# The causal mask enters the score banks by copies on ScalarE and VectorE instead of by a product on TensorE

## The chip, the cores and the metric

The kernel runs on one core of a Trainium2 chip. The metric is the device time of one execution in microseconds (us). Before the change the median of three runs is 2950.63 us (2949.73 to 2951.7).

## The reference, cut to what matters

An audio tower: 64 rows of 2048 samples are cut into 128 tokens of 16 samples, embedded into 256 features, passed through an attention that is near the identity, normalised, and then sent through two transformer layers. Each layer has an attention and a feed-forward part. What the change touches is the attention of the two layers, computed per row of 128 tokens with 8 heads of 64:

```python
q, k = rotary_xpos(l2norm(q) * qs, l2norm(k) * ksc)
sim  = einsum('bhwid,bhwjd->bhwij', q * 8, k)       # scores, 128 x 128 per head
sim  = where(i < j, -max, sim)                      # causal mask
attn = softmax(sim);  out = attn @ v;  x = x + out @ wo
```

The 64 rows are independent windows for this kernel: one row is one window of 128 tokens.

## The kernel before, in words

`front` does the tokenizer and the first attention, `layers` the two transformer layers. In `layers` each engine runs a written-out order of work. `attention_tensor`, `attention_scalar`, `attention_vector`, `attention_pool` and `attention_sync` each have a `body(t, i, u, on)`, which is step t. `on(lag)` says that in step t the engine does its part for row b = t - lag. So one step holds parts of six different rows, in a software pipeline: 64 rows and 5 more steps to drain, first peeled steps, then a loop over four steps at a time, then peeled steps again. Engines meet only through counting semaphores; `need(engine, sem, n)` is a wait for a count. Within an engine all is in order.

PSUM has 8 banks. In the layers' attention, banks 0 and 1 take the projection to q and k, bank 2 the projection to v and later the product of weights and values, banks 3 and 4 the transposes (of q and k, later of the softmax weights), banks 5 and 6 are the score banks `ps_s` (four heads of 128 columns in each, index r), bank 7 takes the transposed input and the output projection.

One step, in each engine's own order:

- TensorE: transpose x of row t (L1215); projection to q and k, then v, for row t-1 (L1202 to L1204, 18 products of 512 columns); output projection of row t-5 (L1244 to L1246); transposes of q and k of row t-2 (L1257); weights times values of row t-4 (L1269); the mask product into both score banks (L1279) and the 16 score products (L1284) of row t-2; transposes of the softmax weights of row t-3 (L1294). L1279 multiplies a 128x128 bf16 identity by the bf16 mask `causal` (four copies of a 128x128 pattern with -1e30 above the diagonal) with `start=True`, and the score products add to it with `start=False`.
- ScalarE: copy of transposed x (L948, L949); four exponentials of row t-3, r = 0 (L937, each with a read of its accumulator); squares of q and k of row t-1 (L957); four exponentials, r = 1; copies v (L965), qT (L970), kT (L972), oT_hi (L977), two ET (L983).
- VectorE: low parts of x (L1068, L1070); reciprocal and scaling of the weights r = 0 (L1059, L1061); the rotary products rot_a (L1079) and rot_b (L1082, two); reciprocal and scaling r = 1; x_new (L1095); sum of squares (L1099) and its clamp ssm (L1101); the row maximum of the scores (L1106) and nbias (L1111); oT_lo (L1118).
- GpSimd: adds rot_a and rot_b (L873), the power -1/2 of ssm (L879), scales k (L883).

The score products wait for qT, kT, and for `exp_done`, that is, for the exponentials of the row before, which read the same banks.

Of the kernel before, what the change touches and what calls it, by code (L numbers as in the profile page):

```python
# [11 lines left out]
ACT = mybir.ActivationFunctionType  # L12
# [28 lines left out]
def need(eng, sem, n):  # L41

    if not isinstance(n, int) or n > 0:
        eng.wait_ge(sem, n)
# [548 lines left out]
def run_from(eng, base, count, depth, body):  # L593

    head = -(-(depth + 2) // 4) * 4  # L600

    def peeled(t):
        body(base + t, (base + t) // 4, t % 4, lambda lag: 0 <= t - lag < count)

    for t in range(head):
        peeled(t)
    with eng.Fori(head // 4, count // 4) as i:
        for u in range(4):
            body(4 * i + (base + u), i + base // 4, u, lambda lag: True)
    for t in range(count, count + depth):  # L610
        peeled(t)
# [95 lines left out]
def layers(nc, c, w, q_scale, k_scale, cos, sin, ln_g, ln_b, b1, xa, xb, out, extra):  # L707
# [4 lines left out]
    with ExitStack() as ctx:  # L712
# [14 lines left out]
        oT_hi = m.sb("oT_hi", [P, KI, P], F32R)  # L727
        oT_lo = m.sb("oT_lo", [P, KI, P], F32R)
# [6 lines left out]
        ps_s = banks[:, 5:7]  # L735
# [5 lines left out]
        s = {n: m.sem(n) for n in (  # L741
            "xT_ps", "xT_hi", "xT_lo", "qk_ps", "v_ps", "squared", "normed", "rn_done", "rot_a", "rot_b", "roped",
            "qk_done", "v_done", "q_ps", "k_ps", "qT_done", "kT_done", "s_ps", "top_done", "nbias_done", "exp_done",
            "rsum_done", "en_done", "e_ps", "et_done", "o_ps", "oT_hi", "oT_lo", "out_ps", "x_done")}

        n = Memory(nc, ctx, "ffn")
        w.forward_home(n)
# [168 lines left out]
        def group_high(act, layer, t, u):  # L916
            for kk in range(KD):
                need(act, f["xT_ps"], KD * t + kk + 1)
                need(act, f["xT_lo"], KD * (t - 1) + kk + 1)
                act.activation(yg[:, kk], ps_T[:, kk], ACT.Identity, bias=b_col[:, layer, kk:kk + 1],  # L920
                               scale=g_col[:, layer, kk:kk + 1]).then_inc(f["xg"], 1)
            for kk in range(KD):
                need(act, f["xg"], KD * t + kk + 1)
                need(act, f["h_ps"], KH * (t - 1))
                act.activation(yT_hi[:, u % 2, kk], yg[:, kk], ACT.Copy).then_inc(f["xT_hi"], 1)

        def attention_scalar(act, layer):
            L = layer * ROWS

            def exps(t, u, r):  # L930
                b, slot = t - 3, (u - 3) % 2
                if r == 0:
                    need(act, s["nbias_done"], b + 1)
                    need(act, s["e_ps"], 2 * b)
                for i in range(HEADS // 2):
                    h = 2 * i + r
                    last = act.activation(E[:, r, i], ps_s[:, r, i * P:(i + 1) * P], ACT.Exp,  # L937
                                          bias=nbias[:, r, i:i + 1], scale=rn[:, slot, h:h + 1],
                                          accum_out=sums[:, r, i:i + 1])
                last.then_inc(s["exp_done"], 1)  # L940

            def body(t, i, u, on):
                step = t - L if isinstance(t, int) else None
                if on(0):

                    need(act, s["xT_ps"], t + 1)
                    need(act, s["v_ps"], t - 1)
                    act.activation(xT_hi[:, u % 2, 0], ps_x[:, 0:P], ACT.Copy).then_inc(s["xT_hi"], 1)  # L948
                    act.activation(xT_hi[:, u % 2, 1, 1:P], ps_x[:, P:2 * P - 1], ACT.Copy).then_inc(s["xT_hi"], 1)  # L949
                if on(3):  # L950
                    exps(t, u, 0)
                if on(1):
                    b = t - 1

                    need(act, s["qk_ps"], b + 1)
                    need(act, s["normed"], 2 * b - 1)
                    act.activation(sq[:].rearrange("p h d -> p (h d)"), ps_qk[:].rearrange("p a n -> p (a n)"),  # L957
                                   ACT.Square).then_inc(s["squared"], 1)
                if on(3):
                    exps(t, u, 1)  # L960
                if on(1):
                    b = t - 1
                    need(act, s["v_ps"], b + 1)
                    need(act, s["o_ps"], b - 3)
                    act.activation(v[:, (u - 1) % 4], ps_v[:], ACT.Copy).then_inc(s["v_done"], 1)  # L965
                if on(2):
                    b = t - 2
                    need(act, s["q_ps"], b + 1)
                    need(act, s["s_ps"], b)
                    act.activation(qT[:].rearrange("p k n -> p (k n)"), ps_q[:], ACT.Copy).then_inc(s["qT_done"], 1)  # L970
                    need(act, s["k_ps"], b + 1)
                    act.activation(kT[:].rearrange("p k n -> p (k n)"), ps_k[:], ACT.Copy).then_inc(s["kT_done"], 1)  # L972
                if on(4):
                    b = t - 4
                    need(act, s["o_ps"], b + 1)
                    need(act, s["out_ps"], b)
                    act.activation(oT_hi[:].rearrange("p k n -> p (k n)"), ps_v[:], ACT.Copy).then_inc(s["oT_hi"], 1)  # L977
                if on(3):
                    b = t - 3
                    need(act, s["o_ps"], b)  # L980
                    for r, src in ((0, ps_q), (1, ps_k)):
                        need(act, s["e_ps"], 2 * b + r + 1)
                        act.activation(ET[:, r].rearrange("p i n -> p (i n)"), src[:], ACT.Copy  # L983
                                       ).then_inc(s["et_done"], 1)
                if step == ROWS + 4:
                    group_high(act, layer, layer * GROUPS, 0)

            run_from(act, L, ROWS, 5, body)

        def forward_scalar(act, layer):  # L990
# [60 lines left out]
        def attention_vector(dve, layer):  # L1051
# [3 lines left out]
            def normalise(t, r):  # L1055
                b = t - 3
                need(dve, s["exp_done"], 2 * b + r + 1)
                need(dve, s["en_done"], 2 * b + r - 1)
                dve.reciprocal(rsum[:, r], sums[:, r]).then_inc(s["rsum_done"], 1)  # L1059
                need(dve, s["rsum_done"], 2 * b + r + 1)  # L1060
                dve.tensor_tensor(E[:, r], E[:, r], rsum[:, r].unsqueeze(2).to_broadcast([P, HEADS // 2, P]),  # L1061
                                  ALU.mult).then_inc(s["en_done"], 1)

            def body(t, i, u, on):
                step = t - L if isinstance(t, int) else None
# [8 lines left out]
                if on(1):  # L1074
                    b = t - 1
# [9 lines left out]
                    last.then_inc(s["rot_b"], 1)  # L1085
                if on(3):
                    normalise(t, 1)
                if step == ROWS + 3:
                    group_statistics(dve, layer * GROUPS, layer * GROUPS // 4, 0)
                if on(5):  # L1090
                    b, hf, slot = t - 5, 2 * i + (u - 5) // 2, (u - 5) % 2
# [4 lines left out]
                if on(1):  # L1096
                    b = t - 1
# [4 lines left out]
                if on(2):  # L1102
                    b, slot = t - 2, u % 2
# [11 lines left out]
                if on(4):  # L1115
                    b = t - 4
# [4 lines left out]
                if step == ROWS + 4:  # L1121
                    group_low(dve, layer * GROUPS, 0)

            run_from(dve, L, ROWS, 5, body)

        def forward_vector(dve, layer):
# [70 lines left out]
        def attention_tensor(pe, layer):  # L1197
# [9 lines left out]
            def body(t, i, u, on):  # L1207
                step = t - L if isinstance(t, int) else None
# [8 lines left out]
                if on(1):  # L1217

                    b, slot = t - 1, (u - 1) % 2
# [15 lines left out]
                if on(5):  # L1235

                    b = t - 5
# [10 lines left out]
                if on(2):  # L1248

                    b, slot = t - 2, u % 2  # L1250
# [9 lines left out]
                if on(4):  # L1260

                    b = t - 4
# [9 lines left out]
                if on(2):  # L1272

                    b = t - 2
                    need(pe, s["qT_done"], b + 1)
                    need(pe, s["kT_done"], b + 1)
                    need(pe, s["exp_done"], 2 * b)
                    for r in range(2):
                        pe.matmul(ps_s[:, r], c["ident_b"][:], c["causal"][:].rearrange("p i n -> p (i n)"),  # L1279
                                  start=True, stop=False, skip_group_check=True)  # L1280
                    for j in range(HEADS // 2):
                        for r in range(2):
                            part = slice(r * HD, (r + 1) * HD)
                            last = pe.matmul(ps_s[:, r, j * P:(j + 1) * P], qT[part, j], kT[part, j], start=False,  # L1284
                                             stop=True, skip_group_check=True)
                    last.then_inc(s["s_ps"], 1)
                if on(3):

                    b = t - 3
# [215 lines left out]
```

## Time and profile before

| | |
|---|---|
| median of 3 runs | 2950.63 us |
| the profiled execution's own time | 2949.1 us |
| its span, first to last instruction | 2947.3 us |
| mean granted TensorE clock | 0.974 of full speed |
| TensorE busy | 2735.2 us (93%) |
| VectorE busy | 2028.5 us (69%) |
| ScalarE busy | 1711.5 us (58%) |
| GpSimd busy | 1416.4 us (48%) |

Matrix products are pipelined, so that their durations overlap; what one costs is read from the distance between starts. The two layers' attentions run from about 724 to 1394 us and from about 1837 to 2515 us of the span. A stretch in which an engine has no idle time is one that this engine paces; whether another engine is close behind is read from that engine's idle time and what ended it.

### The profile page before, as it was taken

The page shows a single profiled execution, that of the slowest core. Times are in us where ns is not written, and L with a number is a line of the kernel's source. Part 1 is how long each engine was busy: PE and PEld are TensorE (multiplying, and loading weights), DVE is VectorE, ACT ScalarE, POOL GpSimd, SP SyncE. Part 2 cuts the span into 40 slices and gives each one's busy share as a digit, 9 for nine tenths or more (in the row PEclk, how much of TensorE's full clock was granted, in tenths as well). Part 3 has the DMA queues.
Part 4 walks back from the last instruction along what each step waited for, and adds up shares of the span by engine and source line. Part 5 has one row for each costly group of instructions (what it writes and reads, how often), then busy time and mean ns, then how long its engine had stood idle before and what let it go on. Part 6 is the DMA issues. An engine that isn't in the chain of part 4 may idle for free.

```text
span 2947.3 us, 68736 instructions
## 1 busy us (share of the span) xinstructions
PE 2735.2 (93%) x23808; PEld 2327.5 (79%) x23808; DVE 2028.5 (69%) x3898; ACT 1711.5 (58%) x4309; POOL 1416.4 (48%) x1338
## 2 busy tenths in 40 slices
PE   6998888994999999998799998899999999699998
PEld 5887777883788888887588887688888888588887
DVE  4665555654888888886565554788888888466664
ACT  3555445552777777776344442677777777344443
POOL 7666666665866666664200001866666666000000
PEclk9999999997999999999899999999999999799999
DMA  1000000012111111111211111111111111122221
GB/s 25 30 29 28 28 28 28 31 50 65 42 38 37 37 37 39 40 39 40 73 55 54 53 52 40 44 38 39 40 38 37 37 37 32 54 82 80 76 76 44
DMA packets 149258, 130.57 MB, mean 44 GB/s; under 512 B 23133, under 2 KB 147327, under 8 KB 149100
## 3 DMA queue, kind: packets, MB, share of 16 engines
q1 hardware_dynamic: 146796, 119.87, 13.5%
q0 software_dynamic: 2304, 8.47, 1.0%
q8 instruction: 114, 1.87, 0.3%
q14 instruction: 44, 0.36, 0.0%
HBM read 77.54 MB, written 50.33 MB: 43 GB/s over the span
## 4 chain that ended last, share of the span: by engine, by line
PE 67%; issue 4%; DMA 2%; POOL 1%; DVE 1%; ACT 1%; SPq 0%; DVEq 0%; POOLq 0%; ACTq 0%
PE const_banks L1202 6%; PE const_banks L1204 6%; PE const_banks L1203 6%; PE const_banks L1315 5%; PE const_banks L1317 5%; PE const_banks L1316 5%; PE const_banks L1284 5%; PE const_banks L1294 4%; PE const_banks L1269 4%; PE const_banks L1257 4%; PE const_banks L1329 2%; PE const_banks L1331 2%; PE const_banks L1330 2%; PE const_banks L1279 2%; PE const_banks L1246 2%
## 5 line engine op out<-in xcount | busy, mean ns | idle before, releaser
L873 POOL TENSOR_TENSOR attn_qk<-attn_rot_a,attn_rot_b 128x1024 f32<-128x1024 f32 x128 | 365.0, 2851 | 470.4 <-PE const_banks L1257 364.5
L937 ACT ACTIVATE attn_E<-const_banks,attn_nbias,attn_rn 128x128 f32<-128x128 f32 x1024 | 456.3, 471 | 3.9 <-DVE attn_nbias L1111 3.7
L879 POOL TENSOR_TENSOR attn_rn<-attn_ssm,const_neg_half 128x16 f32<-128x16 f32 x128 | 373.6, 2919 | 16.5 <-DVE attn_ssm L1101 5.5
L860 POOL TENSOR_TENSOR ffn_rstd<-ffn_var,const_neg_half 128x4 f32<-128x4 f32 x32 | 32.3, 1010 | 725.8 <-DVE ffn_var L1036 725.8
L1202 PE MATMUL const_banks<-weights_w_hi,attn_xT_hi 128*128 128x512 f32 x768 | 314.9, 410 | 4.7 <-DVE attn_rot_b L1082 4.1
L1315 PE MATMUL const_banks<-ffn_xT_hi,ffn_w_hi 128*128 128x512 f32 x704 | 283.6, 403 | 25.2 <-DVE ffn_gated L1135 21.6
L1204 PE MATMUL const_banks<-weights_w_hi,attn_xT_lo 128*128 128x512 f32 x768 | 303.1, 395 | 0.0
L1203 PE MATMUL const_banks<-weights_w_lo,attn_xT_hi 128*128 128x512 f32 x768 | 301.0, 392 | 0.0
L1135 DVE SCALAR_TENSOR_TENSOR ffn_gated<-const_banks,ffn_b_col,ffn_gate 128x512 f32<-128x512 f32 (+1 forms) x192 | 143.7, 748 | 225.1 <-ACT ffn_gate L1004 217.7
L1317 PE MATMUL const_banks<-ffn_xT_hi,ffn_w_lo 128*128 128x512 f32 x704 | 279.9, 398 | 0.0
L1316 PE MATMUL const_banks<-ffn_xT_lo,ffn_w_hi 128*128 128x512 f32 x704 | 279.8, 397 | 0.0
L983 ACT ACTIVATE attn_ET<-const_banks 128x512 f32<-128x512 f32 x256 | 139.5, 595 | 210.7 <-PE const_banks L1294 210.7
L1004 ACT ACTIVATE ffn_gate<-const_banks,ffn_b_col 128x512 f32<-128x512 f32 x160 | 110.0, 688 | 228.9 <-PE const_banks L1317 228.8
L937 ACT ACTIVATION_READ_ACCUMULATOR attn_E<-const_banks,attn_nbias,attn_rn 128x1 f32 x1024 | 224.5, 219 | 0.0
L1061 DVE TENSOR_TENSOR attn_E<-attn_E,attn_rsum 128x512 f32<-128x512 f32 x256 | 209.9, 820 | 8.8
L1014 ACT ACTIVATE ffn_h_hi<-ffn_gated 128x512 fp32r<-128x512 f32 x160 | 101.2, 632 | 158.8 <-DVE ffn_gated L1135 158.8
L1329 PE MATMUL const_banks<-ffn_w_hi,ffn_h_hi 128*128 128x256 f32 x640 | 182.0, 284 | 6.1 <-DVE ffn_h_lo L1143 6.1
L1331 PE MATMUL const_banks<-ffn_w_hi,ffn_h_lo 128*128 128x256 f32 x640 | 181.5, 284 | 0.0
L1330 PE MATMUL const_banks<-ffn_w_lo,ffn_h_hi 128*128 128x256 f32 x640 | 181.5, 284 | 0.0
L1079 DVE TENSOR_TENSOR attn_rot_a<-const_banks,attn_cos_s 128x1024 f32<-128x1024 f32 x128 | 156.6, 1224 | 34.7 <-ACT attn_sq L957 33.6
L1315 PEld LDWEIGHTS const_banks<-ffn_xT_hi,ffn_w_hi 128*128 128x128 f32 x704 | 134.2, 191 | 52.5 <-DVE ffn_gated L1135 22.5
L368 ACT ACTIVATE ident_E<-const_banks 128x1024 f32<-128x1024 f32 x128 | 124.1, 1022 | 83.4 <-PE const_banks L551 83.4
(171 smaller groups left out, 7945.9 us busy)
## 6 DMA issues: line engine op xcount, KB each, us to landing
attn_x_<-xa SPq DMA_DIRECT2D x128, 128.0 KB, 2.1
attn_x_res<-xa SPq DMA_DIRECT2D x128, 128.0 KB, 2.1
xb<-attn_x_new SPq DMA_DIRECT2D x128, 128.0 KB, 1.7
ffn_x_<-xb SPq DMA_DIRECT2D x32, 512.0 KB
h<-ident_h SPq DMA_DIRECT2D x64, 128.0 KB, 1.7
xa<-ident_n SPq DMA_DIRECT2D x64, 128.0 KB, 1.7
xa<-ffn_x_new SPq DMA_DIRECT2D x16, 512.0 KB, 3.6
ffn_add<-h SPq DMA_DIRECT2D x16, 512.0 KB, 7.0
```

Of the source, the lines that this page charges most:

```text
L873: pool.tensor_tensor(qk[:, slot].rearrange("p a n -> p (a n)"), rot_a[:].rearrange("p a h d -> p (a h d)"), rot_b[:].rearrange("p a h d -> ...
L879: pool.tensor_tensor(rn[:, slot], ssm[:], c["neg_half"][:], ALU.pow).then_inc(s["rn_done"], 1)
L937: last = act.activation(E[:, r, i], ps_s[:, r, i * P:(i + 1) * P], ACT.Exp, bias=nbias[:, r, i:i + 1], scale=rn[:, slot, h:h + 1], accum_o ...
L1202: pe.matmul(out_, xT_hi[:, slot, k], w.w_hi[:, k, cols], start=(k == 0), stop=False)
L1203: pe.matmul(out_, xT_hi[:, slot, k], w.w_lo[:, k, cols], start=False, stop=False)
L1204: last = pe.matmul(out_, xT_lo[:, slot, k], w.w_hi[:, k, cols], start=False, stop=(k == KD - 1))
L1315: pe.matmul(dst, w.w1_hi[:, kk, at], yT_hi[:, slot, kk], start=(kk == 0), stop=False)
L1316: pe.matmul(dst, w.w1_hi[:, kk, at], yT_lo[:, slot, kk], start=False, stop=False)
L1317: last = pe.matmul(dst, w.w1_lo[:, kk, at], yT_hi[:, slot, kk], start=False, stop=(kk == KD - 1))
L1329: pe.matmul(dst, h_hi[:, slot, k, tok], w.w2_hi[:, k], start=(k == 0), stop=False)
L1330: pe.matmul(dst, h_hi[:, slot, k, tok], w.w2_lo[:, k], start=False, stop=False)
L1331: pe.matmul(dst, h_lo[:, slot, k, tok], w.w2_hi[:, k], start=False, stop=False)
```

## The change

The mask product is kept for the first row of each layer only. For the other 63 rows of each layer, ScalarE copies the mask into score bank 0 behind the four exponentials r = 0 (semaphore `seed0`), and VectorE copies it into score bank 1 behind the scaling r = 1 (semaphore `seed1`). Each copy waits for the exponentials that read its bank. TensorE's score products wait for both copies and add to what lies in the banks.

```diff
-            "rsum_done", "en_done", "e_ps", "et_done", "o_ps", "oT_hi", "oT_lo", "out_ps", "x_done")}
+            "rsum_done", "en_done", "e_ps", "et_done", "o_ps", "oT_hi", "oT_lo", "out_ps", "x_done", "seed0", "seed1")}
+        mask = c["causal"][:].rearrange("p i n -> p (i n)")
...
                 if on(3):
                     exps(t, u, 0)
+                    if on(2):
+                        need(act, s["exp_done"], 2 * (t - 3) + 1)
+                        act.activation(ps_s[:, 0], mask, ACT.Copy).then_inc(s["seed0"], 1)
...
                 if on(3):
                     normalise(t, 1)
+                    if on(2):
+                        need(dve, s["exp_done"], 2 * (t - 3) + 2)
+                        dve.tensor_copy(ps_s[:, 1], mask).then_inc(s["seed1"], 1)
...
                     need(pe, s["exp_done"], 2 * b)
-                    for r in range(2):
-                        pe.matmul(ps_s[:, r], c["ident_b"][:], c["causal"][:].rearrange("p i n -> p (i n)"),
-                                  start=True, stop=False, skip_group_check=True)
+                    if step == 2:
+                        for r in range(2):
+                            pe.matmul(ps_s[:, r], c["ident_b"][:], mask, start=True, stop=False, skip_group_check=True)
+                    else:
+                        need(pe, s["seed0"], b - layer)
+                        need(pe, s["seed1"], b - layer)
```

## Rows read from the trace of the kernel before

**Rows 1.** Windows: busy time and count of each engine, clock, DMA share.

```profile
core 0: us, PE busy (x) PEld busy (x) DVE busy (x) ACT busy (x) POOL busy (x), PEclk, DMA share, GB/s
800.00:1350.00 550.00, 550.00 (x4352) 462.78 (x4351) 465.47 (x797) 426.68 (x1326) 362.58 (x160) 1.00 0.13 38
...
1001.98:1012.34 10.36, 10.36 (x85) 8.71 (x84) 8.98 (x16) 8.05 (x26) 6.95 (x4) 1.00 0.12 38
```

**Rows 2.** Chain of waits in order of time, score products: start, duration.

```profile
752.30 1.09 PE const_banks L1284 x16
762.66 1.09 PE const_banks L1284 x16
...
1354.22 1.09 PE const_banks L1284 x16
...
1906.86 1.09 PE const_banks L1284 x16
...
2487.02 1.09 PE const_banks L1284 x16
```

**Rows 3.** Timeline of TensorE in one step: start, duration, work.

```profile
1010.71 1.09 PE L1269 MATMUL const_banks<-attn_ET,attn_v 128*64 128x128 f32 x16
1011.74 0.60 PE L1279 MATMUL const_banks<-const_causal,const_ident_b 128*128 128x512 bf16 x2
1012.27 1.16 PE L1284 MATMUL const_banks<-attn_kT,attn_qT 64*128 64x128 f32 x16
```

**Rows 4.** Timeline of VectorE over one round.

```profile
1008.27 1.23 DVE L1079 TENSOR_TENSOR attn_rot_a<-const_banks,attn_cos_s 128x1024 f32<-128x1024 f32 x1
...
1010.81 0.69 DVE L1061 TENSOR_TENSOR attn_E<-attn_E,attn_rsum 128x512 f32<-128x512 f32 x1
1011.42 0.42 DVE L1095 TENSOR_TENSOR attn_x_new<-const_banks,attn_x_res 128x256 f32<-128x256 f32 x1
1011.75 1.21 DVE L1099 TENSOR_REDUCE attn_ss<-attn_sq 128x16 f32<-128x1024 f32 x1
1012.99 0.76 DVE L1101 TENSOR_SCALAR attn_ssm<-attn_ss 128x16 f32<-128x16 f32 x1
1013.67 1.21 DVE L1106 TENSOR_REDUCE attn_neg_top<-const_banks 128x8 f32<-128x1024 f32 x1
1014.91 0.17 DVE L1111 TENSOR_TENSOR attn_nbias<-attn_neg_top,attn_rn 128x8 f32<-128x8 f32 x1
1015.00 0.68 DVE L1118 TENSOR_TENSOR attn_oT_lo<-const_banks,attn_oT_hi 128x512 fp32r<-128x512 f32 x1
...
1018.63 1.22 DVE L1079 TENSOR_TENSOR attn_rot_a<-const_banks,attn_cos_s 128x1024 f32<-128x1024 f32 x1 [0.22 <-ACT attn_sq L957]
```

**Rows 5.** Timeline of ScalarE over the same round.

```profile
1010.38 0.60 ACT L970 ACTIVATE attn_qT<-const_banks 128x512 f32<-128x512 f32 x1
1010.87 0.59 ACT L972 ACTIVATE attn_kT<-const_banks 128x512 f32<-128x512 f32 x1
...
1015.34 0.48 ACT L937 ACTIVATE attn_E<-const_banks,attn_nbias,attn_rn 128x128 f32<-128x128 f32 x1
...
1016.99 0.25 ACT L937 ACTIVATION_READ_ACCUMULATOR attn_E<-const_banks,attn_nbias,attn_rn 128x1 f32 x1
1017.57 1.03 ACT L957 ACTIVATE attn_sq<-const_banks 128x1024 f32<-128x1024 f32 x1 [0.34 <-PE const_banks L1204]
```

**Rows 6.** Timeline of GpSimd, the addition in the same round.

```profile
1010.82 2.90 POOL L873 TENSOR_TENSOR attn_qk<-attn_rot_a,attn_rot_b 128x1024 f32<-128x1024 f32 x1 [3.14 <-PE const_banks L1257]
```

**Rows 7.** One line of the kernel: durations ns, least/median/greatest.

```profile
L1101 DVE TENSOR_SCALAR attn_ssm<-attn_ss x128: 233/757/2080, 716.4 to 2497.7; 128x16 f32<-128x16 f32 x128
```

**Rows 8.** Timeline where one engine waits for another, late in layer 1.

```profile
1367.15 0.17 DVE L1111 TENSOR_TENSOR attn_nbias<-attn_neg_top,attn_rn 128x8 f32<-128x8 f32 x1
...
1367.35 0.46 ACT L937 ACTIVATE attn_E<-const_banks,attn_nbias,attn_rn 128x128 f32<-128x128 f32 x1
...
1389.48 0.69 DVE L1061 TENSOR_TENSOR attn_E<-attn_E,attn_rsum 128x512 f32<-128x512 f32 x1
...
1390.22 0.66 PE L1294 MATMUL const_banks<-const_ident,attn_E 128*128 128x128 f32 x4 [0.82 <-DVE attn_E L1061]
```

**Rows 9.** Groups by line: the mask product, and its idle time before.

```profile
L1279 PE MATMUL const_banks<-const_causal,const_ident_b 128*128 128x512 bf16 x256 | 78.7, 390 | 3.1 <-issue 1.5 <-ACT attn_kT L972 0.8 <-ACT attn_qT L970 0.8
```

## The prediction

> **What bounds the kernel now.** I read the windows first, since the busy shares of the whole span mix stages. In the attention of layer 1, from 800 to 1350 us, TensorE is busy for 550.00 of 550.00 us at full clock, VectorE for 465, ScalarE for 427, GpSimd for 363 [rows 1]. One step there takes exactly 10.36 us, and TensorE is busy for all of it. The chain of waits says the same in another way: its longest pieces are the score products, one every 10.36 us, from 752.30 to 1354.22 in layer 1 (58 steps, 10.38 in the mean) and from 1906.86 to 2487.02 in layer 2 (56 steps of 10.36) [rows 2]. So in some 118 steps (these 114, and one or two at each end that look alike) the step is as long as TensorE's own stream of work.
>
> The second thing to see is how far behind the others are, and busy shares don't tell that. VectorE's busy 8.98 us in a step look like 1.4 us of room. But VectorE and ScalarE form a round with each other, which I read from their timelines and count from the start of rot_a, called R (1008.27) [rows 4, 5]:
>
> - scaling r = 1 starts at R+2.54, x_new at R+3.15, the sum of squares at R+3.48, ssm at R+4.72, the maximum at R+5.40, nbias at R+6.64 [rows 4];
> - the exponentials r = 0 need nbias. They start at R+7.07 and their last accumulator read ends at 1017.24, R+8.97, that is 1.90 later [rows 5];
> - ScalarE then idles for 0.34 us, until TensorE's projection ends; the squares start at R+9.30 and last 1.03; rot_a of the next step follows at R+10.36, 1.06 after the squares began [rows 4, 5].
>
> Of the 10.36 us only the 0.34 before the squares are idle in this ScalarE part. The round VectorE, ScalarE, VectorE is thus nearly as long as TensorE's stream, and its room is what counts when work is moved to those two engines.
>
> **What is removed.** TensorE's two mask products. Their 390 ns each [rows 9] overlap, so I take the distance of starts: weights times values starts at 1010.71, the mask product at 1011.74, the score products at 1012.27 [rows 3]. The mask costs 0.53 us a step. Without it TensorE's stream would be 10.36 - 0.53 = 9.83 us. If nothing else were in the way, 118 x 0.53 = 63 us would be gained.
>
> **What is added on VectorE.** A copy of 128x512 from SBUF into PSUM behind the scaling r = 1. No row of before shows this operation. The nearest is oT_lo, the same number of columns with one operand in PSUM: 0.68 us [rows 4]; scaling of 512 columns takes 0.69 and lets the next one start 0.61 after its own start (1010.81 to 1011.42). Bounds: 0.42 (x_new, 256 columns) and 1.23 (rot_a, 1024 columns). I take 0.68, and 0.60 until the next start. It starts where x_new does now, at R+3.15, since the wait for the exponentials r = 1 was already met for the reciprocal ahead of it. Its end is R+3.83.
>
> Queued behind it: x_new (now R+3.75), the sum of squares (R+4.08), ssm (R+5.32). Here something gives. ssm has 16 columns and takes 0.76 us in the round shown, 0.757 in the median and 0.233 at the least [rows 7]. It ends at 1013.75, just after GpSimd's addition (1010.82 + 2.90 = 1013.72, R+5.45) [rows 4, 6]. I read this as ssm being held until the addition is done. If so, an ssm that starts 0.6 later is held only 0.13 us, and the maximum starts at R+5.40 to R+5.47, as before or 0.07 later. Nbias starts at R+6.64 to R+6.71, and exponentials can start 0.20 after that (1367.15 to 1367.35) [rows 8]: at most R+6.91. So VectorE's copy is nearly hidden in the round, by ssm's held time. If that cover didn't exist, it would cost its 0.60.
>
> The Trainium skill has a rule that bears on this (SBUF — State Buffer, Who interferes with whom): VectorE and GpSimd share one pair of ports as an exclusive lock, and a one-source operation such as tensor_scalar takes it in its two-port mode. The row of ssm agrees. Its other half speaks against the change, since a copy is such an operation too; that case is the fourth rival below.
>
> **What VectorE's copy does to TensorE.** The score products now wait for it. A product was released 0.05 us after VectorE's end (1389.48 + 0.69 to 1390.22) [rows 8]; I take that, with 0.14 as the upper bound. The scores start at R+3.88, where before they start at 1012.27, R+4.00 [rows 3]. TensorE, done with weights times values at about R+3.4 to R+3.5 [rows 3], idles until then. It gains nothing of the 0.53 but 0.12. From the scores' start to the exponentials r = 0 there were 3.07 us (1012.27 to 1015.34) [rows 3, 5], through the transposes and ScalarE's copies ET and xT_hi. So this way gives R+6.95, slightly later than the way over nbias. I take R+6.95.
>
> **What is added on ScalarE.** A copy of the same shape, between the exponentials r = 0 and the squares. Nearest: qT, 128x512, 0.60 us, next start 0.49 later (1010.38 to 1010.87) [rows 5]. The source here is SBUF and the target PSUM, which no row shows; bounds are 0.25 (a 1-column read) and 1.03 (1024 columns). I take 0.50 to the next start. Before it the wait for its own exponentials, which ends the overlap of neighbours: 0.03 to 0.12, I take 0.07 (nbias to exponential released 0.03 after nbias' end, rows 8). So: exponentials R+6.95, end 1.90 later R+8.85, copy at R+8.92, squares R+9.42. TensorE's projection isn't in the way: the squares that waited for it began 5.30 us after the scores' start (1012.27 to 1017.57) [rows 3, 5], and nothing between the two changes on TensorE, so it would allow them at R+9.18. The next rot_a: 9.42 + 1.06 = R+10.48. Queued behind ScalarE's copy are the squares, the exponentials r = 1, v, qT and kT; they all move with R, and kT stays ready 0.7 before the scores.
>
> **The sum.** The round is 10.48 us with the chosen values; with the other ends of the small ones (0.14 for 0.05, 0.12 for 0.07) it is 10.62. I take 10.50: 0.14 us more a step than before, 118 x 0.14 = 17 us. The first and last steps of a layer don't run at TensorE's pace; there each copy stands on the path of ScalarE or VectorE with about 0.5 us and the mask product goes with 0.53. I put 2 us on all of them. Profiled execution: 2949.1 + 19 = 2968 us. The median of before lies 1.5 us above that execution, so the forecast is 2970 us, 0.65% slower. The removed work was on the bounding engine and its removal is real, but the added work closes a round that had 0.34 us of room.
>
> **Rivals.**
>
> 1. *The copies are cheaper than I take them, and the round stays under TensorE's old step.* For: the round has held time and idle time, both unequally sized from step to step. With the copies at their lower bounds (0.42 and 0.25) the round is max(6.69, 6.84) + 1.90 + 0.07 + 0.20 + 1.06 = 10.07 (0.20 being ScalarE's 0.25 less the overlap of neighbours). Against: the rows of 512 columns are all near 0.6 to 0.7. I price it at 10.20: -0.16 x 118 = -19, 2932 us. The full gain (9.83) would give 2888 us and needs the round to shrink, for which I see nothing.
> 2. *The two effects cancel*, a step of 10.31 to 10.40: 2945 to 2956 us.
> 3. *Nothing is absorbed* (this ends slower, by much): ssm takes 0.7 for a reason of its own, and both copies lie in the round in full. Round now: 6.64 + 0.20 + 1.90 + 1.06 = 9.80; and 0.60 + 0.57 more are 10.97, or 11.1 with the upper wait times. It decides as soon as their sum is above the 0.56 by which 9.80 is under 10.36. 0.7 x 118 = +83, 3034 us. Here belong longer copies too: at both upper bounds (1.23 and 1.03) the scores' way gives 3.15 + 1.23 + 0.14 + 3.07 = R+7.59 and the round 7.59 + 1.90 + 0.12 + 0.92 + 1.06 = 11.59, or 3096 us. Against it: ssm's least of 0.233 and its end right behind the addition's.
> 4. *VectorE's copy is held by GpSimd's addition*, as ssm is. The addition runs from R+2.55 to R+5.45. The copy would end at R+6.1, the scores start at R+6.2, the exponentials at R+9.25, the next rot_a at R+12.8: +2.4 x 118 = +285, 3236 us. Against it: the sum of squares (1.21, as long as the maximum, which reads PSUM) and x_new (0.42) run beside that addition and are not stretched [rows 4, 6], and the target here is a PSUM bank. The Trainium skill says so too (VectorE: DVE Perf Modes, Why PSUM operands drop a tier: an operand in PSUM excludes the two-port mode).
>
> That the copies don't do what they say (scores overwrite the mask instead of adding to it) would not change the time.
>
> **How the numbers follow.** Forecast (step 10.40 to 10.75): 0.55. Rival 1: 0.20. Rival 2: 0.10. Rival 3: 0.11. Rival 4: 0.04. A measurement of this kernel tells 0.2%, 6 us, from no change. Slower by more: 0.55 + 0.11 + 0.04 = 0.70; within: 0.10; faster: 0.20. The range leaves out rival 4, the far half of rival 3 and the near half of rival 1: 2936 to 3024. The forecast's own range is 2955 to 2998.
>
> **What would show it.** In the changed kernel's steady steps: score products every 10.50 us; TensorE idle about 0.5 us ahead of them, released by VectorE's copy; VectorE's copy 0.68 and ScalarE's 0.60; ssm near 0.25 to 0.35 instead of 0.76, with the maximum starting about 5.4 after rot_a; no idle time between ScalarE's copy and the squares; the addition on GpSimd still 2.9. Wrong if TensorE is still busy without a gap (rival 1), if ssm keeps 0.7 (rival 3), or if VectorE's copy lasts 2 us (rival 4).

## The result: 1.3% slower, and the profile after

The changed kernel takes 2989.93 us in the median of 4 runs (2987.27 to 2992.65), the kernel before in the same session 2950.18 us (2949.71 to 2951.7): 1.0134 times the time, 95% interval 1.0116 to 1.0151. Forecast were 2970 us, slower, in a range of 2936 to 3024. The direction and the mechanism were right; the loss is 40 us, twice the 20 that were forecast.

Windows, kernel after: the stretch of [rows 1] again.

```profile
core 0: us, PE busy (x) PEld busy (x) DVE busy (x) ACT busy (x) POOL busy (x), PEclk, DMA share, GB/s
800.00:1350.00 550.00, 512.64 (x4131) 446.24 (x4131) 451.50 (x829) 439.63 (x1338) 353.37 (x155) 1.00 0.12 37
```

TensorE, without a gap before, now has 37 us idle in 550, and no other engine is above 452. Nothing is full any more, and the stretch is slower: that is what a round of waits looks like. The waits of the whole span name its parts (engine, line, waited for; us in total, times, longest):

```profile
PE const_banks L1294 <- DVE const_banks L1094: 79.2, 124, 2.3
DVE attn_rot_a L1083 <- ACT attn_sq L961: 70.1, 125, 4.9
```

The chain of waits, which before was one long piece of TensorE (67% of the span), is now 34% TensorE, 15% issue, 13% ScalarE, 10% VectorE:

```profile
PE 34%; issue 15%; ACT 13%; DVE 10%; DMA 2%; POOL 1%; DVEq 0%; ACTq 0%; SPq 0%; POOLq 0%
```

One round, timeline of the kernel after; R is the start of rot_a, 1000.74 (L numbers are those of the changed file):

```profile
1000.74 1.22 DVE L1083 TENSOR_TENSOR attn_rot_a<-const_banks,attn_cos_s 128x1024 f32<-128x1024 f32 x1 [0.46 <-ACT attn_sq L961]
...
1003.29 2.89 POOL L874 TENSOR_TENSOR attn_qk<-attn_rot_a,attn_rot_b 128x1024 f32<-128x1024 f32 x1 [3.56 <-DVE attn_rot_b L1086]
...
1003.89 0.69 DVE L1094 CAST const_banks<-const_causal 128x512 f32<-128x512 bf16 x1
...
1004.72 1.16 PE L1294 MATMUL const_banks<-attn_kT,attn_qT 64*128 64x128 f32 x16 [0.57 <-DVE const_banks L1094]
...
1006.06 0.17 DVE L1108 TENSOR_SCALAR attn_ssm<-attn_ss 128x16 f32<-128x16 f32 x1
1006.15 1.22 DVE L1113 TENSOR_REDUCE attn_neg_top<-const_banks 128x8 f32<-128x1024 f32 x1
...
1007.86 0.48 ACT L938 ACTIVATE attn_E<-const_banks,attn_nbias,attn_rn 128x128 f32<-128x128 f32 x1
...
1009.78 0.60 ACT L955 ACTIVATE const_banks<-const_causal 128x512 f32<-128x512 bf16 x1
...
1010.32 1.01 ACT L961 ACTIVATE attn_sq<-const_banks 128x1024 f32<-128x1024 f32 x1
...
1011.55 1.23 DVE L1083 TENSOR_TENSOR attn_rot_a<-const_banks,attn_cos_s 128x1024 f32<-128x1024 f32 x1 [0.66 <-ACT attn_sq L961]
```

It is to be read against [rows 3] to [rows 6]. VectorE's copy stands at R+3.15, where x_new stood. The scores start at R+3.98, where before they started at R+4.00: TensorE's saved 0.53 us are gone in the 0.57 of idle time in brackets. ssm takes 0.17 instead of 0.76 and the maximum starts at R+5.41, as before (R+5.40): VectorE's copy is hidden there. ScalarE's copy is not hidden: the squares follow it at once, at R+9.58 instead of R+9.30.

Over steps 8 to 60 of each layer the mean step was 10.36 us before and is 10.66 in layer 1, 10.64 in layer 2. The kernel's loop does four steps a turn. In layer 1 three steps of 10.62 are followed by one of 10.81, in layer 2 by one of 10.71, and the round shown is one of 10.81. The profiled executions differ by 43.5 us (spans 2990.8 and 2947.3), as follows, from the starts of rot_a and the last x_new of each layer:

```
                        before    after   difference
up to layer 1            712.8    717.1     +4.3
layer 1, steps 0 to 8     88.3     91.7     +3.4
         steps 8 to 60   538.7    554.6    +15.9
         rest             70.1     71.7     +1.6
layer 2, steps 0 to 8     88.7     91.6     +2.9
         steps 8 to 60   538.7    553.2    +14.5
         rest             70.0     71.5     +1.5
```

In the stretch of the first line no instruction differs. The granted clock from 500 to 700 us was 0.94 in the execution of before and 0.91 in this one. The ten kernels of the experiments, which don't differ there either, have between 714.5 and 718.0 us on this line, all above the one profile of before. So I don't count its 4.3 us as work of the change, but why they arise stays open. Of the other 40 us, 30 lie in steps 8 to 60 and 9 outside them.

### The profile page after: what moved, and what is told of

The parts are those of the page before. It is cut to its first block, busy times and chain, and to the rows that moved or that the text cites. A ratio compares the mean times of both kernels' runs of the same rounds, so it can differ in the third digit from the quotient of the medians.

```text
span 2990.8 us, 68720 instructions
## 1 busy us (share of the span) xinstructions
PE 2688.4 (90%) x23554; PEld 2326.1 (78%) x23556; DVE 2028.5 (68%) x4024; ACT 1776.8 (59%) x4435; POOL 1416.8 (47%) x1338
## 4 chain that ended last, share of the span: by engine, by line
PE 34%; issue 15%; ACT 13%; DVE 10%; DMA 2%; POOL 1%; DVEq 0%; ACTq 0%; SPq 0%; POOLq 0%
ACT attn_E L938 6%; DVE attn_rot_b L1086 5%; PE const_banks L1325 5%; PE const_banks L1327 5%; PE const_banks L1326 5%; PE const_banks L1294 5%; ACT attn_sq L961 4%; DVE const_banks L1094 3%; PE const_banks L1304 3%; PE const_banks L1339 2%; PE const_banks L1341 2%; PE const_banks L1340 2%; DMA ffn_x_<-xb 2%; ACT attn_ET L987 1%; PE const_banks L1200 1%
## 5 line engine op out<-in xcount | busy, mean ns | idle before, releaser
L1294 PE MATMUL const_banks<-attn_kT,attn_qT 64*128 64x128 f32 x2048 | 151.0, 286 | 80.7 <-DVE const_banks L1094 79.2
L1294 PEld LDWEIGHTS const_banks<-attn_kT,attn_qT 64*128 64x128 f32 x2048 | 129.8, 190 | 108.6 <-issue 106.4
```

## The experiments

Ratios are to the kernel before, run beside each. "Step" is the mean step between 900 and 1300 us of that kernel's trace; the times after R, to the start of the scores and of the squares, are medians of the same stretch, added up from the timelines and good to 0.03 us. In most kernels the steps differ over the four steps of a loop turn, so the squares' time, their duration of 1.03 and the step don't add up exactly.

```
kernel                                time us  ratio (95%)                step   scores  squares
before                                2950     1                          10.36   4.00    9.30
changed                               2989.93  1.0134 (1.0116 to 1.0151)  10.66   3.98    9.58
e1 ScalarE's copy alone               2964.27  1.0043 (1.0026 to 1.0060)  10.41   3.66    9.33
e2 VectorE's copy alone               2993.98  1.0142 (1.0125 to 1.0158)  10.68   4.29    9.58
e2b the same, product before the wait 2946.66  0.9985 (0.9975 to 0.9994)  10.29   3.89    9.17
e3 both, ScalarE's behind kT          2961.01  1.0030 (1.0020 to 1.0040)  10.38   3.98    9.27
e4 e3 and the exchange on TensorE     2930.45  0.9924 (0.9907 to 0.9940)  10.08   4.03    8.68
e5 changed and the exchange           2995.07  1.0152 (1.0135 to 1.0169)  10.64   4.40    9.54
e6 before and the exchange            2968.63  1.0061 (1.0043 to 1.0080)  10.44   4.89    9.37
e7 ScalarE's alone, behind kT         2928.96  0.9924 (0.9907 to 0.9941)  10.13   3.73    9.00
e8 e7 and a short fill on VectorE     2924.55  0.9912 (0.9895 to 0.9928)  10.13   3.73    9.00
e9 e7 and a long fill on VectorE      2988.09  1.0128 (1.0111 to 1.0145)  10.65   3.34    9.18
```

**e1, ScalarE's copy alone.**

```diff
                 if on(3):
                     normalise(t, 1)
-                    if on(2):
-                        need(dve, s["exp_done"], 2 * (t - 3) + 2)
-                        dve.tensor_copy(ps_s[:, 1], mask).then_inc(s["seed1"], 1)
...
                         need(pe, s["seed0"], b - layer)
-                        need(pe, s["seed1"], b - layer)
+                        pe.matmul(ps_s[:, 1], c["ident_b"][:], mask, start=True, stop=False, skip_group_check=True)
```

> ScalarE's copy alone: VectorE's copy is gone, TensorE multiplies the mask into bank 1 only (one product of 512 columns), bank 0 is copied by ScalarE. Theory A (a round through both engines: scores, exponentials r = 0, ScalarE's copy, squares, rotary products, and back to the scores): TensorE's stream would be 10.10 us a step, but the round R+6.88, +1.89, +0.03, +0.54, +1.04 gives 10.38 to 10.45. So 2950 to 2962 us, against about 2950 of before. Rival B (only VectorE's copy costs, because the scores wait for it, and ScalarE's copy lies in idle time): 10.10 us a step, 2950 - 31 = 2919 us.

Measured: step 10.41, 2964 us. Theory A, with the step inside its 10.38 to 10.45 and the time 2 us above. TensorE has 0.27 us a step less to do and gains nothing by it. The squares start at R+9.33, where before they started at R+9.30.

**e2, VectorE's copy alone.**

```diff
-                    if on(2):
-                        need(act, s["exp_done"], 2 * (t - 3) + 1)
-                        act.activation(ps_s[:, 0], mask, ACT.Copy).then_inc(s["seed0"], 1)
...
-                        need(pe, s["seed0"], b - layer)
                         need(pe, s["seed1"], b - layer)
+                        pe.matmul(ps_s[:, 0], c["ident_b"][:], mask, start=True, stop=False, skip_group_check=True)
```

> VectorE's copy alone: ScalarE's is gone, TensorE multiplies the mask into bank 0, bank 1 is copied by VectorE. Theory A: the scores start at R+3.98 as in the changed kernel, exponentials r = 0 at R+7.12, ready at R+9.01, but the squares then wait for TensorE's projection, 5.30 after the scores, R+9.28, and the next rot_a comes at R+10.34. So 10.34 to 10.40 us a step, 2946 to 2956 us: each copy alone costs nothing, the two together 0.3 us a step. Rival B (the loss is VectorE's copy and the scores' wait for it): the step stays near 10.65 and the time near 2985 us.

Measured: 2994 us, step 10.68. That looks like rival B, but the scores start at R+4.29 and not at R+3.98: my edit had put the mask product, which needs no copy, behind the wait, and so on the path. 4.28 + 5.30 + 1.06 is 10.64. The run thus can't tell Theory A from rival B. **e2b** changes only that order:

```diff
-                        need(pe, s["seed1"], b - layer)
                         pe.matmul(ps_s[:, 0], c["ident_b"][:], mask, start=True, stop=False, skip_group_check=True)
+                        need(pe, s["seed1"], b - layer)
```

> VectorE's copy alone again, but TensorE issues the mask product for bank 0 ahead of its wait for VectorE's copy, not behind it; behind it, the product of 0.27 us stood on the path and the step was 10.64 at the least, which is 4.28 + 5.30 + 1.06. Theory A (round over TensorE: rot_a to scores 3.98, scores to squares 5.30, squares to rot_a 1.06): 10.34 us a step, 2948 to 2960 us. Rival B (VectorE's copy costs by itself, by what it shifts on VectorE): still 10.6 or more, 2985 us or more.

Measured: 2947 us, step 10.29 (10.24 in the median), 1 us under Theory A's range and far from rival B. One line's place is worth 47 us, and VectorE's copy costs nothing by itself. In e2 the scores started 0.45 us after the copy's end, here 0.06 after it; the product of 0.27 is the larger part of the difference, and the quicker start is the rest. The timeline of e2b, scores and copy:

```profile
1004.72 0.69 DVE L1091 CAST const_banks<-const_causal 128x512 f32<-128x512 bf16 x1
...
1005.46 1.16 PE L1291 MATMUL const_banks<-attn_kT,attn_qT 64*128 64x128 f32 x16 [0.22 <-DVE const_banks L1091]
```

Here the scores start 0.05 us after the copy's end (1005.41); in the changed kernel it was 0.14 (1004.58 to 1004.72). Taken without rounding it is 0.056 in e2b and 0.147 in the changed kernel, nearly the same in every step.

**e3, ScalarE's copy moved.**

```diff
                 if on(3):
                     exps(t, u, 0)
-                    if on(2):
-                        need(act, s["exp_done"], 2 * (t - 3) + 1)
-                        act.activation(ps_s[:, 0], mask, ACT.Copy).then_inc(s["seed0"], 1)
...
                     act.activation(kT[:].rearrange("p k n -> p (k n)"), ps_k[:], ACT.Copy).then_inc(s["kT_done"], 1)
+                    if on(3):
+                        need(act, s["exp_done"], 2 * (t - 3) + 1)
+                        act.activation(ps_s[:, 0], mask, ACT.Copy).then_inc(s["seed0"], 1)
```

> Both copies as in the changed kernel, but ScalarE makes its copy behind kT (where it idles 0.25 us before oT_hi) and not ahead of the squares. Theory A: the copy leaves the round; kT ends at R+3.2, the copy at R+3.8, no later than VectorE's copy lets the scores go (R+3.98). Squares at R+9.28, when TensorE's projection is done; step 10.34 to 10.40, 2946 to 2956 us. Rival B (the scores' wait for VectorE's copy is the whole loss, wherever ScalarE copies): 10.65, 2985 us. Rival C (ScalarE's copy costs wherever it stands, since oT_hi and ET come later): near 10.6 too.

Measured: step 10.38 (10.33 in the median), 2961 us. The steady step is Theory A's; rivals B and C fall, since the same two copies with the same wait on TensorE cost 0.28 us a step less. The time is 5 us above the range: steps 0 to 8 took 91.2 and 91.0 us, as in the changed kernel, where the kernel before took 88.3 and 88.7. Why the first steps lose this wasn't tried; e2b has it too (90.8, 90.5), e7 hardly (88.3, 89.2). One round of e3, R = 1004.96:

```profile
1007.85 0.61 ACT L976 ACTIVATE const_banks<-const_causal 128x512 f32<-128x512 bf16 x1
1008.10 0.69 DVE L1094 CAST const_banks<-const_causal 128x512 f32<-128x512 bf16 x1
...
1008.93 1.16 PE L1294 MATMUL const_banks<-attn_kT,attn_qT 64*128 64x128 f32 x16 [0.64 <-DVE const_banks L1094]
...
1014.23 1.03 ACT L958 ACTIVATE attn_sq<-const_banks 128x1024 f32<-128x1024 f32 x1 [0.27 <-PE const_banks L1211]
...
1015.29 1.23 DVE L1083 TENSOR_TENSOR attn_rot_a<-const_banks,attn_cos_s 128x1024 f32<-128x1024 f32 x1
```

The scores start at R+3.97 and still wait for VectorE. The squares start at R+9.27, and what they wait for is TensorE's projection again.

**e4, e3 with an exchange on TensorE**: transposes of the softmax weights ahead of the scores.

```diff
                 if on(2):
+                    need(pe, s["qT_done"], t - 1)
+                    need(pe, s["kT_done"], t - 1)
+                if on(3):
+                    b = t - 3
+                    need(pe, s["et_done"], 2 * b)
+                    for r, dst in ((0, ps_q), (1, ps_k)):
...
+                        last.then_inc(s["e_ps"], 1)
+                if on(2):
 
                     b = t - 2
-                    need(pe, s["qT_done"], b + 1)
-                    need(pe, s["kT_done"], b + 1)
                     need(pe, s["exp_done"], 2 * b)
```

> As the kernel with ScalarE's copy behind kT, and on TensorE the transposes of the softmax weights (0.93 us) are moved ahead of the score products, into the time in which TensorE waits for the two copies. Theory A: TensorE doesn't wait any more; its stream is 9.83, scores at R+4.4, done R+5.6, nbias R+6.85, exponentials R+7.05 to R+8.94, squares R+8.9; by ScalarE the step would be 9.96, but the scaling r = 0 on VectorE is held by GpSimd's scaling of k (ends R+9.64) to R+10.15, so 10.0 to 10.2: 2908 to 2932 us, faster than before by about 1%. Rival B (the scores are now 0.5 us later and everything behind them, too): 10.6 or more, 2980 us.

Measured: step 10.08, 2930 us, 0.8% faster than before. What ends the step is the held scaling, as expected; timeline of e4 at the end of a round:

```profile
1010.88 1.04 POOL L884 TENSOR_TENSOR attn_qk<-attn_qk,attn_rn 128x512 f32<-128x512 f32 x1
1011.05 1.03 ACT L958 ACTIVATE attn_sq<-const_banks 128x1024 f32<-128x1024 f32 x1
...
1011.50 0.97 DVE L1065 TENSOR_TENSOR attn_E<-attn_E,attn_rsum 128x512 f32<-128x512 f32 x1
...
1012.40 1.21 DVE L1083 TENSOR_TENSOR attn_rot_a<-const_banks,attn_cos_s 128x1024 f32<-128x1024 f32 x1
```

The squares are done at 1012.08, and rot_a starts only at 1012.40, behind the scaling. That takes 0.97 us instead of 0.69, ending 0.55 after GpSimd's scaling of k (1011.92). It is the next bound after TensorE's stream and the round through ScalarE, and the prediction has no such term: in the kernel before this scaling ended at R+10.14 in the median, 0.54 to 0.55 behind GpSimd's scaling of k in all 122 steps in which it started beside it, and rot_a started 0.08 before its end in 35 of 40 steps of e4. 10.14 - 0.08 is 10.06: with GpSimd's work as it is, the 9.83 of TensorE's shorter stream was out of reach by this estimate.

**e5 and e6, the exchange without the moved copy, and without any copy.** The edit is e4's, on the changed kernel and on the kernel before.

> The changed kernel with the two parts of TensorE's order exchanged (transposes of the weights ahead of the scores), ScalarE's copy left ahead of the squares. Theory A: TensorE doesn't wait any more, but the round through ScalarE stays: exponentials R+7.05, +1.87, +0.03, +0.54, +1.07 give R+10.56. So 2970 to 2985 us, nearly the changed kernel's time, although TensorE's wait ahead of the scores is gone. Rival B (TensorE's wait is the loss): 10.1 us a step, 2930 us.

> The kernel before with the exchange alone, mask products kept on TensorE. Theory A: TensorE's stream is unchanged at 10.36, but the scores end 0.93 later than they did, so the maximum waits for them; exponentials R+7.55, squares R+9.40, next rot_a R+10.46: 10.36 to 10.50 us a step, 2950 to 2968 us. So what is gained by both together isn't the exchange. Rival B (the exchange is a gain of its own): 2930 to 2940 us.

Measured: e5 2995 us, step 10.64, ten over its range but clearly not rival B: TensorE no longer waits ahead of the scores, and the time stays. TensorE's idle time has only moved: from 800 to 1350 us it is 29.5 us, all ahead of weights times values. e6 2969 us, 0.6 us above its range, step 10.44: the maximum waits for the scores, as expected. So the exchange is worth nothing alone. It isn't needed for a gain either: e7, below, has none. What e4 and e7 share is that ScalarE copies, but outside the round.

**e7, ScalarE's copy alone, behind kT.** On e3:

```diff
-                    if on(2):
-                        need(dve, s["exp_done"], 2 * (t - 3) + 2)
-                        dve.tensor_copy(ps_s[:, 1], mask).then_inc(s["seed1"], 1)
...
+                        pe.matmul(ps_s[:, 1], c["ident_b"][:], mask, start=True, stop=False, skip_group_check=True)
                         need(pe, s["seed0"], b - layer)
-                        need(pe, s["seed1"], b - layer)
```

> ScalarE's copy alone, behind kT; TensorE multiplies the mask into bank 1 ahead of its waits. Theory A: TensorE's stream is 10.10; the scores start when ScalarE's copy is done, R+3.9; squares R+9.2, next rot_a R+10.26: 10.24 to 10.32 us a step, 2935 to 2947 us. Rival B (any copy on ScalarE lengthens its part by its own 0.5 us): 10.5 or more, 2965 us or more.

Measured: 2929 us, step 10.13. Faster than Theory A's 10.24 to 10.32, and 6 us under its range: the scores started at R+3.73, not R+3.9. The copy begins 0.47 after kT's start, and TensorE isn't stalled at all. Its window, as in [rows 1]:

```profile
core 0: us, PE busy (x) PEld busy (x) DVE busy (x) ACT busy (x) POOL busy (x), PEclk, DMA share, GB/s
800.00:1350.00 550.00, 550.00 (x4391) 472.42 (x4389) 480.13 (x816) 460.62 (x1417) 372.40 (x164) 1.00 0.13 39
```

TensorE is again busy throughout, with one product of 0.27 less a step: 10.36 before, some 10.1 now. The scaling r = 0 is as near here: it ends at R+10.14, and in half of the steps (19 of 39) rot_a follows it at once, 0.08 before its end.

**e8 and e9, how much VectorE can take.** On e7, a fill of a tile that nobody reads, of 512 and of 1152 columns:

```diff
                     dve.tensor_tensor(x_new[:, slot], ps_x[:, D:2 * D], x_res[:, slot], ALU.add).then_inc(s["x_done"], 1)
+                    dve.memset(fill[:], 0.0)
```

> The kernel with ScalarE's copy alone, behind kT (10.13 us a step), and one more VectorE operation behind x_new that nobody waits for: a fill of 512 columns of an unused tile, some 0.55 to 0.6 us. It tests whether ssm's held time absorbs work on VectorE. Theory A (ssm is held until GpSimd's addition ends at R+5.45, so work that ends before costs nothing): ssm starts near R+5.3, the maximum still at R+5.40, step 10.1 to 10.2, time within 4 us of 2929. Rival B (ssm lasts 0.7 for a reason of its own; the round takes the fill in full): the maximum at R+6.0, step about 10.6, 2985 us.

> The same with a fill of 1152 columns, some 1.2 to 1.3 us. Theory A: the held time of 0.7 is used up, ssm starts at R+5.95 and is not held, the maximum at R+6.1, exponentials R+7.55, squares R+9.4, next rot_a R+10.45: the step is 10.4 to 10.55, 0.3 to 0.4 above the kernel with the short fill, 2965 to 2980 us. Rival B: twice the short fill's loss.

Timeline of e8 and, below, of e9, ssm and its neighbours:

```profile
1000.48 0.48 DVE L1101 MEMSET attn_fill<- 128x512 f32 x1
1000.88 1.16 DVE L1105 TENSOR_REDUCE attn_ss<-attn_sq 128x16 f32<-128x1024 f32 x1
1002.08 0.27 DVE L1107 TENSOR_SCALAR attn_ssm<-attn_ss 128x16 f32<-128x16 f32 x1
```

```profile
1001.29 1.02 DVE L1101 MEMSET attn_fill<- 128x1152 f32 x1 [0.19 <-issue]
1002.23 1.16 DVE L1105 TENSOR_REDUCE attn_ss<-attn_sq 128x16 f32<-128x1024 f32 x1
1003.42 0.17 DVE L1107 TENSOR_SCALAR attn_ssm<-attn_ss 128x16 f32<-128x16 f32 x1
```

With the short fill the step is 10.13, as without (ratio 0.9912 and 0.9924, intervals overlap); ssm is shorter by what the fill took, and the maximum starts at R+5.39 in both. With the long one the maximum starts at R+5.96, 0.57 later, and the step is 10.65, 0.52 longer: what goes beyond the held time comes back nearly in full. The time of e8, 2925 us, is 4.4 us from 2929, just outside the 4 us that were expected, and on the fast side. Rival B is out, for the short fill cost nothing. I had put e9 at 10.4 to 10.55, by way of ScalarE. It is 10.65 because ssm late also makes GpSimd's power and scaling of k late, and those hold the scaling r = 0 on VectorE, which ended at R+10.71 (R+10.14 in e7), right ahead of rot_a. Timeline of e9 at the end of a round:

```profile
1006.66 1.04 POOL L885 TENSOR_TENSOR attn_qk<-attn_qk,attn_rn 128x512 f32<-128x512 f32 x1
...
1006.80 1.03 ACT L959 ACTIVATE attn_sq<-const_banks 128x1024 f32<-128x1024 f32 x1
...
1007.25 1.01 DVE L1066 TENSOR_TENSOR attn_E<-attn_E,attn_rsum 128x512 f32<-128x512 f32 x1
...
1008.18 1.21 DVE L1084 TENSOR_TENSOR attn_rot_a<-const_banks,attn_cos_s 128x1024 f32<-128x1024 f32 x1
```

The squares are done at 1007.83; rot_a follows the scaling.

## Why the prediction was right, and the terms it mis-sized

**What bounds the kernel.** Right: TensorE's stream, with a round through ScalarE and VectorE 0.34 us behind. TensorE went from 550.00 busy to 512.64 of 550 and time was lost.

**What is removed** (0.53 us a step, 9.83 without the mask). The size is borne out by e7, where half of it (0.27) is removed and the step falls by 0.23, though the scaling r = 0 is as near there as TensorE. In the changed kernel all of it became idle time ahead of the scores.

**VectorE's copy.** Right in place, duration (0.68 taken, 0.685 in the median) and in what hides it: ssm. The line of the kernel after, against [rows 7]:

```profile
L1108 DVE TENSOR_SCALAR attn_ssm<-attn_ss x128: 174/174/1486, 720.7 to 2541.8; 128x16 f32<-128x16 f32 x128
```

e8 and e9 show the cover and its end. The forecast had 0.25 to 0.35 for ssm; it took 0.17, started at R+5.32 and so ended just behind the addition, as before. That it is GpSimd's addition which holds ssm rests on their ends: ssm took 0.757 in the kernel before and 0.27 in e8, where it starts 0.5 later, and in both it ended 0.03 to 0.04 us behind the addition in all but 2 of 128 rows; in e9, where it starts behind the addition's end, it took 0.17. The Trainium skill's rule on the shared ports (SBUF — State Buffer, Who interferes with whom) agrees. A kernel without the addition wasn't run.

**The scores' wait.** Mis-sized: I took 0.05 from VectorE's end to TensorE's start, and it was 0.147, at the upper bound of 0.14. That bound stood in the working without a row. Between scores and exponentials it was 3.13 and not 3.07; 0.06 of it lies between the end of the transposes and ScalarE's first copy ET, 0.10 where before it was 0.04. It is 0.04 in the four kernels in which ScalarE doesn't copy the mask (before, e2, e2b, e6) and 0.10 in the eight in which it does; why isn't shown. So the exponentials r = 0 start at R+7.11, not R+6.95. These 0.16 us account for the whole error of the usual step, which is 0.14.

**ScalarE's copy.** Its own duration was right: 0.60 in all 126. Its wait took 0.03 instead of 0.07, the next start came 0.54 after its own instead of 0.50. The squares start at R+9.58 instead of R+9.42. And from the squares' end to rot_a it wasn't 0.03 in every step: in the 54 steps of layer 1 from 800 to 1380 us 13 had 0.22 to 0.24, where the kernel before had 0.12 in 13 of 56 and 0.03 in nearly all others. In layer 2 the changed kernel had 0.12, too. It is every fourth step, and always the first of a turn of the loop over four steps; where this time goes wasn't looked into. So the step's terms give

```
                             taken   measured
scores                       R+3.88   R+3.98
exponentials r = 0           R+6.95   R+7.11
ScalarE's copy               R+8.92   R+9.04
squares                      R+9.42   R+9.58
next rot_a, usual            R+10.48  R+10.62
            mean                      R+10.66
```

The working named 10.62 as the value with the waits at their upper ends, and then took 10.50. With 10.65 the 118 steps give 34 us instead of 17. That is most of what was missing. That the usual step is 10.62 as well is in part luck: the wait on TensorE came out as its upper bound has it, but the other 0.05 of that sum was in ScalarE's wait, which was short, and the 0.06 ahead of ET wasn't in the sum at all.

**The layers' ends.** Mis-sized: 2 us taken. The 9 us outside steps 8 to 60 hold 14 of the forecast's 118 steps, which at 0.29 us each make 4; so 5 us are left for the ends. They lie in steps 5 and 6 above all (in layer 1 13.53 and 11.05 us, before 12.06 and 10.06).

**The rivals.** Rival 1 (copies cheap enough) fell: they cost 0.60 and 0.685 us, as taken. Its outcome, a faster kernel, came in e4 and e7 with the same cost a copy and another place for ScalarE's. Rival 2 (the effects cancel) fell with the step of 10.66. Rival 3 (nothing absorbed) fell by ssm's 0.174. Rival 4 (VectorE's copy held by GpSimd's addition) fell: 0.680 to 0.689 us in all 126 copies, 122 of them beside the addition. The Trainium skill's rule (VectorE: DVE Perf Modes, Why PSUM operands drop a tier) agrees with that.

## What to carry to other kernels

An engine that is busy all the time is one bound; the next one is the shortest room in the rounds of waits, and busy shares don't show it. Before moving work from the full engine to a half-idle one, follow one round in the timeline and find where the receiver idles: the same copy of 0.6 us on ScalarE cost 0.3 us a step ahead of the squares and nothing behind kT. And an instruction that does not need a wait belongs ahead of it: here that one line was worth 47 us.

## What the runs showed of the hardware

- TensorE started 0.14 us after VectorE's end when it had stood idle for 0.57 us, and 0.05 us after it in e2b, where a product had been issued just ahead of the wait and the idle time was 0.22 us. Which of the two makes the difference wasn't tried.
- The time from the end of the squares on ScalarE to rot_a on VectorE took few values: 0.03 us in most steps, but in the first step of each turn of the loop 0.12 in the kernel before (13 of 56 steps) and 0.22 to 0.24 in the changed kernel's layer 1 (13 of 54).
- VectorE's scaling of the weights, which reads two operands in SBUF, took 0.69 us when it started ahead of GpSimd's instruction. Started 0.24 to 0.64 us ahead of the end of GpSimd's scaling of k, it ended 0.54 to 0.55 us behind that end and so took 0.79 to 1.19 us (122 steps of the kernel before).
- A copy of 128x512 from bf16 in SBUF to f32 in PSUM took 0.60 us on ScalarE and 0.685 us on VectorE, as their copies and sums of 512 columns that read PSUM.
